# A two-layer gated attention and expert kernel: four small changes of order inside the attention turns

## The reference, cut to what matters

```python
x = x + tanh(g_xattn[0]) * cross_attention(layernorm(x), ctx)            # 16 heads of 32
x = x + tanh(g_ffn[0])   * experts(layernorm(x))                         # 128 experts, groups of 32 tokens
x = x + tanh(g_xattn[1]) * cross_attention(layernorm(x), ctx, mask, biases)
x = x + tanh(g_ffn[1])   * (sigmoid(xr @ Wr.T) * (relu(xk @ Wk.T)**2 @ Wv.T))

def cross_attention(q_in, ctx):
    q, k, v = q_in @ Wq.T + bq, ctx @ Wk.T + bk, ctx @ Wv.T + bv
    probs = softmax(q @ k.T / sqrt(32))                                  # per head, over 120 context tokens
    return (probs @ v) @ Wo.T + bo                                       # biases in the second layer only
```

## Time and profile before

| | |
|---|---|
| median of three runs | 1439.5 us |
| profiled execution, own time | 1443.21 us |
| its span, first to last instruction | 1441.4 us |
| mean granted TensorE clock | 0.962 |
| busy: PE, DVE, ACT, POOL | 1297.9, 906.9, 571.3, 426.9 us |
| one steady turn, first layer / second layer | 46.2 / 50.2 us |

### The profile page before, as it was taken

How to read it: one execution, slowest core, us unless ns; L and a number is a source line. 1 busy time by engine, 2 the same in 40 slices (tenths; PEclk the granted TensorE clock), 3 DMA queues, 4 the chain that set the end, 5 groups by cost and what they waited for, 6 DMA issues and landing times.

```text
span 1441.4 us, 28299 instructions
## 1 busy us (share of the span) xinstructions
PE 1297.9 (90%) x10624; PEld 920.2 (64%) x10624; DVE 906.9 (63%) x1583; ACT 571.3 (40%) x1025; POOL 426.9 (30%) x351
## 2 busy tenths in 40 slices
PE   6976899999999879786989999999995799999997
PEld 5765567766777667522446656765673677777776
DVE  6986267666666446554546756666573577777762
ACT  3331444344533455443452342343233333333331
POOL 3200235432551100000341321231131644444440
PEclk9987899999999999998999999999997899999999
DMA  9962532445233566999892552464202311111100
GB/s 332 286 184 84 167 123 80 134 166 158 85 93 119 191 187 190 334 390 367 324 362 93 174 190 81 134 202 138 94 20 89 117 59 58 58 58 58 56 29 33
DMA packets 128852, 219.55 MB, mean 152 GB/s; under 512 B 27286, under 2 KB 48278, under 8 KB 124686
## 3 DMA queue, kind: packets, MB, share of 16 engines
q1 hardware_dynamic: 128782, 218.58, 44.9%
HBM read 135.67 MB, written 82.88 MB: 152 GB/s over the span
## 4 chain that ended last, share of the span: by engine, by line
PE 53%; issue 19%; DVE 13%; ACT 6%; DMA 4%; POOL 3%; SPq 1%; DVEq 0%; POOLq 0%; ACTq 0%
PE b L154 9%; PE b L156 8%; PE b L155 8%; PE b L1464 3%; PE b L1639 3%; PE b L1917 3%; PE b L1640 3%; PE b L1641 3%; DVE f_mix L2132 2%; PE b L1561 2%; PE b L1950 2%; PE b L1436 2%; PE b L1569 2%; ACT a_pr L1066 2%; ACT e_gt L1836 1%
## 5 line engine op out<-in xcount | busy, mean ns | idle before, releaser
L1066 ACT ACTIVATE a_pr<-b 120x512 f32<-120x512 f32 x256 | 134.0, 603 | 124.6 <-PE b L1464 124.6
L1232 DVE TENSOR_REDUCE a_mx<-b 128x4 f32<-128x480 f32 x256 | 151.9, 652 | 4.6 <-PE b L1436 4.5
L995 POOL TENSOR_TENSOR a_atl<-a_pvs,a_ath 128x512 fp32r<-128x512 f32 x64 | 80.7, 1292 | 187.6 <-ACT a_ath L1112 187.6
L1639 PE MATMUL b<-a_woh,a_ath 128*128 128x512 f32 x256 | 105.8, 413 | 5.0 <-POOL a_atl L995 5.0
L154 PE MATMUL b<-a_xth,a_wqh 128*128 128x512 f32 x256 | 105.5, 412 | 4.0 <-DVE a_wql L775 4.0
L955 POOL TENSOR_TENSOR a_rstd<-a_ve,a_mhalf 128x4 f32<-128x4 f32 x16 | 16.2, 1012 | 311.1 <-DVE a_ve L1181 311.1
L1436 PE MATMUL b<-a_kbd,a_qh 128*128 128x480 f32 x256 | 87.3, 402 | 21.0 <-DVE a_mx L1232 20.7
L155 PE MATMUL b<-a_xtl,a_wqh 128*128 128x512 f32 x256 | 102.5, 400 | 0.0
L156 PE MATMUL b<-a_xth,a_wql 128*128 128x512 f32 x256 | 102.4, 400 | 0.0
L1640 PE MATMUL b<-a_wol,a_ath 128*128 128x512 f32 x256 | 102.3, 400 | 0.0
L1641 PE MATMUL b<-a_woh,a_atl 128*128 128x512 f32 x256 | 102.2, 399 | 0.0
(11 more groups left out here) (219 smaller groups left out, 3160.6 us busy)
## 6 DMA issues: line engine op xcount, KB each, us to landing
a_rp<-s_rp SPq DMA_DIRECT2D x128, 256.0 KB, 4.5
s_x<-a_x SPq DMA_DIRECT2D x16, 1024.0 KB, 4.2
s_rp<-e_chosen SPq DMA_DIRECT2D x16, 1024.0 KB, 7.9
s_rp<-e_xc SPq DMA_DIRECT2D x16, 1024.0 KB, 7.8
kv_xb<-in_x SPq DMA_DIRECT2D x8, 1024.0 KB, 8.7
a_xr<-in_x_t SPq DMA_DIRECT2D x8, 1024.0 KB, 6.6
a_x<-in_x SPq DMA_DIRECT2D x8, 1024.0 KB, 8.3
s_xn<-a_xn SPq DMA_DIRECT2D x8, 1024.0 KB, 4.8
```

What stands on the lines that cost most here:

```text
L995: pool.tensor_tensor(quarter(atl, q), quarter(pvs, q), f(quarter(ath, q)), ALU.subtract).then_inc(a_lo, 1)
L1066: act.activation(pr[:, h % RING, :], bank[k][0:S2, :], ACT.Exp, scale=SCALE)\
L1232: dve.tensor_reduce(mx[:, t, :, r], bank[k][:, 0:HJ * S2].rearrange("p (a s) -> p a s", a=HJ), AX.X, ALU.max).then_inc(free[k], 1)
L1639: pe.matmul(out, ath[:, m, cols], woh[:, m, :], start=(m == 0), stop=False)
```

## The change

Four edits, all of order. On GpSimd, `add_bias` waits once, for all four normed tiles, instead of before each addition for its own. On ACT, in both layers, the sixteenth exponential goes ahead of the copy of the third group's values. On DVE, in both layers and in all turns but the last, the first two maxima of group 1 go ahead of the low part of the fourth query chunk. On PE, in the second layer, merge tiles 2 and 3 go ahead of `values(0)`. No instruction is added or removed except three of four waits.

```diff
--- before.py
+++ after.py
@@ -956,8 +956,8 @@
 
         def add_bias(j):
 
+            pool.wait_ge(normed, NT * (j + 1))
             for t in range(NT):
-                pool.wait_ge(normed, NT * j + t + 1)
                 pool.tensor_tensor(xs[:, place_of(j), t], xs[:, place_of(j), t], bo[:, :], ALU.add)\
                     .then_inc(bo_added, 1)
 
@@ -1087,10 +1087,9 @@
             if merge and last:
                 after[0].transposed(act, None, (2, 3))
                 after[0].mixes_high(act, 0, 0, (0, 1))
-            for h in range(12, 15):
+            for h in range(12, 16):
                 exp(h)
             values(2)
-            exp(15)
             if tail:
                 second_norm(i, (2, 3))
             if merge and first_turn(i):
@@ -1348,8 +1347,9 @@
             if not last:
                 queries(j, (1, 2))
                 maxima(i, 0)
+                maxima(i, 1, (0, 1))
                 queries(j, (3,))
-                maxima(i, 1)
+                maxima(i, 1, (2, 3))
                 maxima(i, 2)
             for t in range(NT):
                 k, uses = WV[t % 2]
@@ -1587,14 +1587,14 @@
                 merge_tile(i, i + 1, 0)
                 merge_tile(i, i + 1, 1)
             scores(i, i, 1)
+            if merging:
+                merge_tile(i, i + 1, 2)
+                merge_tile(i, i + 1, 3)
             values(0)
             if merge and last_:
                 pe.wait_ge(free["t"], TB.n(B - 2, "mt", 0) + 1)
                 pe.wait_ge(free["w"], W.n(B - 2, "o", 1) + 1)
                 after[0].transposes(pe, None, (0, 1))
-            if merging:
-                merge_tile(i, i + 1, 2)
-                merge_tile(i, i + 1, 3)
             scores(i, i, 2)
             values(1)
             if merge and last_:
```

## The result

The changed kernel took 1417.33 us in the median of 4 runs (1414.85 to 1420.2), the kernel before 1438.49 in 4: a ratio of 0.9855 with a 95% interval of 0.9818 to 0.9893. The interval of the second set excludes the sum (16.4 of 1439.5 is a ratio of 0.989); that of the first alone doesn't.

A forecast was written before the change was run, and what follows sets the result against it. TensorE's instruction list plus its waits was taken to bound attention turns. Waits of 6.7 + 7.3 + 2.4 = 16.4 us were to go, so 1439.5 - 16.4 = 1423.1 us, with an 8-in-10 range of 1418 to 1431.

The forecast's parts named there:

- What bounds the kernel: Attention layers' middle turns: each lasts as long as TensorE's instruction list plus its waits; reordering can change only the waits.
- Bias and merge, one wait: Second layer: both edits aim at TensorE's wait for normed tiles, gains don't add; 6.7 us, bounds 0 and 8.3.
- Maxima: Both layers: two second maxima ahead of the fourth queries' rest remove TensorE's waits for maxima; 7.3 us, bounds 0 and 7.3.
- Exponentials: First layer: sixteenth exponential ahead of the values' copy removes TensorE's wait before the sums; 2.4 us, bounds 0 and 3.8.
- Rival A: Maxima edit pays nothing because DVE becomes the limit some tiles later; time 1430.4 us; chance 0.09.
- Rival B: Moved bias additions on GpSimd hold up DVE's rounding of the reciprocal sums; 7.7 us, time 1430.8; chance 0.06.
- Rival C: Second layer: merge tiles 2 and 3, 1.9 us nearer their loads, wait for data; 33 us, time 1456; chance 0.02.
- Rival D: Clock dips around the attention layers take some gain back, 8 us of matmuls falling in low stretches; time 1431; chance 0.10.

The follow-up runs named there:

- the second set: Changed kernel run again for more rounds against the kernel before: 1417.52 us against 1439.79, ratio 0.9839 (0.982 to 0.9859).
- a wait per bank: Changed kernel, but each score matmul waits for its own bank instead of all four at the head of the group: 1417.19 and 1416.89 us, ratios 0.9852 and 0.9835.

## Why the mechanism was forecast right, and its size wrong

- *What bounds the kernel*: right. TensorE's list and its waits set the turn; every gain was a TensorE wait that went.
- *Bias and merge, one wait*: right, down to either edit being enough (49.11 and 48.97 alone; 48.19 and 48.06 with the other left out). The size was 1.11 us a turn for 1.04, and the order of the merge tiles gave 0.14 where 0 was taken: 7 x 0.21 = 1.5 us too little, with all seven turns taken alike. In turn 0, where 0.5 us was taken, TensorE's idle time ahead of the transposes and the reciprocal sums went from 0.9 + 1.1 to 0.3 + 0.7 us, about 1.0 less.
- *Maxima*: the mechanism was right, and this is the failing step. The term "4.4 + 2.9 = 7.3 us" took the shown idle as the cost, and even named 7.3 its upper bound. Alone the edit shortened turns by 0.91 and 0.68, 7 x 1.59 = 11.1 us: 3.8 of the missing 6. In its place the runs show that the wait costs what it takes from start to start, with the late successor: 0.90 and 0.67 where 0.63 and 0.41 were shown idle.
- *Exponentials*: 0.27 a turn taken, 0.38 measured alone, 0.8 us too little over seven turns, by the same error.
- Together 1.5 + 3.8 + 0.8 = 6.1, and 16.4 + 6.1 = 22.5 against 21.2 and 22.3 measured in the medians. The upper bounds were built from the same idle times: those for the norm (8.3 against 7 x 1.25 = 8.8) and the maxima (7.3 against 11.1) lay below the true size, and so the low end of the range was set too high. That the median missed the range by only 0.7 us is owed to the 2 us that the range allowed for the spread of runs.
- *Rival A* didn't occur: with the maxima edit alone the full gain came.
- *Rival B* didn't occur in a steady turn of any kernel: the rounding took 0.23 us in all of them. That holds with the bias edit alone too, where the prediction had it hit because it priced the additions 0.6 us too long. In turn 0 of the changed kernel the rounding took 0.67 us and TensorE waited 0.7, less than the 1.18 and 1.1 before; without the merge edit the collision there was worse than before.
- *Rival C* didn't occur: no wait for merge data in the turns. Its price was also too high: the 14.1 us of the earlier trace rows count two of the waits twice, once for the weight load (8.2 us in 4) and once for the matmul behind it (5.9 us in 2).
- *Rival D* isn't seen: the stretch from the first layer's eighth L1581 to the second's first is 265.4 us before and 265.8 after, at a mean granted clock of 0.94 in both, and what follows the last one is 322.2 and 322.4. In the twelve profiles the former varies from 263.4 to 271.0 us without a pattern by edit, so an effect of a few us could hide there.
- The profiled executions differ by 28.3 us, more than the medians. Of that 22.4 lies between the first and the eighth L1581 of the two layers, and 6.5 ahead of the first layer's first L1581, at 172.8 us before and 166.3 after, where the mean granted clock was 0.89 and 0.94. The second profile of the changed kernel has this L1581 at 171.3, and the others have it between 166.5 and 172.6: nearly all of the 6.5 is a difference between executions and not the work of the edits. The medians don't rest on it.

## What to carry to other kernels

The idle time of a pipelined matmul queue starts at the shown end of the last matmul, which here is later than the moment the next could have started. Cost a wait from start to start, and one matmul further, against the same instructions where nothing waits: here that was 1.07 to about 1.65 times the idle shown. It was most where the matmul before overlapped its successor most (0.16 us) and the wait was short, and least for the long wait behind value matmuls (an overlap of 0.07). And count a wait as gone only when the turn is shorter: with a wait per bank the table lost all of it, the turn a quarter.

## What the runs showed that I had not expected

- The maxima matmul that had waited delays its successor: 0.32 us instead of 0.21 from start to start, at an unchanged granted clock of 1.00. The wait need not be the cause as such. The transposes behind the norm's wait took no longer for it (1.89 us with and without), and the first query matmul behind the value matmuls has its successor 0.34 behind it with nothing waited for.
- The last eight matmuls of a merge tile took 0.88 us from their start to the next instruction's where sums followed, and 1.00 where scores or another tile did. Not explained.
- A TensorE wait of 2.0 us in one turn was followed by 3.4 us at the lower clock level, which cost 1.4 us more (bias edit alone). One of 2.1 us at the same place in another kernel was not.
- One VectorE rounding of 128 columns took 0.23 us alone, 1.18 and 1.93 us beside GpSimd's low parts of the output weight, of 1.27 us each. The Trainium skill's page "SBUF — State Buffer", section "Who interferes with whom", has the loser block for a whole instruction of the other. The 1.18 agrees with that, as 0.95 lost is less than one such instruction. The 1.7 us lost in the 1.93 are more than one such instruction, so more than one wait of that kind must lie in it, or something else besides. No run here tells which.
